# Expert biases as a float16 product of split weights, gelu rows handled by halves, and gate weights prepared one expert earlier

## What is computed

```
x = x + attention(layernorm(x))
h = layernorm(x)                                    # [tokens, 128]
gates = h @ router_w + router_b                     # 8 experts, the 2 best are kept
comb = softmax over those 2, zero for the others    # [tokens, 8]
shared = (sum over 2 experts of gelu(h @ sw1 + sb1) @ sw2 + sb2) / 2
moe = sum over 8 experts of comb[e] * (gelu(h @ w1[e] + b1[e]) @ w2[e] + b2[e])
x = x + shared + moe
```

## Time and profile before

| | us |
|---|---|
| median of 3 runs | 2149.64 |
| lowest and highest | 2147.13, 2152.54 |
| the profiled execution | 2150.59 |
| its span, first to last instruction | 2147.1 |
| PE busy in the span | 2082.1 (97%) |
| DVE, ACT, POOL busy | 1637.8, 1513.3, 1161.0 |

### The profile page before, as it was taken

One profiled execution on the slowest core, in us unless ns is written; L12 is line 12 of the kernel. 1 busy time (PEld: TensorE's weight loads), 2 busy tenths in 40 slices (PEclk: granted clock), 3 DMA queues, 4 the chain that ended last, 5 costly groups with the idle time before them and its releaser, 6 DMA issues.

```text
span 2147.1 us, 88171 instructions
## 1 busy us (share of the span) xinstructions
PE 2082.1 (97%) x37442; PEld 1544.8 (72%) x37442; DVE 1637.8 (76%) x3856; ACT 1513.3 (70%) x3304; POOL 1161.0 (54%) x1104
## 2 busy tenths in 40 slices
PE   3999999999999999999999999999998999999998
PEld 1777777777777777777777777777775777777776
DVE  4787787788778878977887787788875676677675
ACT  3666676666676676767666776766656888888887
POOL 5454546356354644544563455454415677777676
PEclk8999999999999999999999999999999999999999
DMA  5112211321221123123112211222112212212210
GB/s 139 33 55 66 74 55 45 86 65 54 62 79 55 45 66 81 49 59 89 48 53 66 75 55 55 76 62 58 44 55 23 30 20 24 29 20 24 29 20 11
DMA packets 255681, 114.48 MB, mean 53 GB/s; under 512 B 142218, under 2 KB 251156, under 8 KB 255348
## 3 DMA queue, kind: packets, MB, share of 16 engines
q1 hardware_dynamic: 255348, 109.60, 21.0%
HBM read 83.34 MB, written 8.39 MB: 43 GB/s over the span
## 4 chain that ended last, share of the span: by engine, by line
PE 84%; ACT 5%; POOL 4%; issue 3%; SPq 1%; DVE 1%; DMA 1%; ACTq 0%; POOLq 0%; DVEq 0%
PE ps L1276 21%; PE ps L1211 11%; PE ps L1296 10%; PE ps L1306 8%; PE ps L1218 8%; PE ps L1229 7%; POOL probs_t L545 3%; ACT probs L692 2%; PE ps L1458 2%; PE ps L1441 2%; PE ps L1443 2%; PE ps L1442 2%; PE ps L1460 2%; PE ps L1459 2%; PE ps L1314 1%
## 5 line engine op out<-in xcount | busy, mean ns | idle before, releaser
L624 ACT ACTIVATE probs<-ps,neg_max 128x512 f32<-128x512 f32 x1024 | 690.5, 686 | 352.2 <-DVE neg_max L819 352.1
L819 DVE TENSOR_REDUCE neg_max<-ps 128x1 f32<-128x512 f32 x1024 | 635.5, 682 | 151.7 <-PE ps L1218 147.3
L463 POOL TENSOR_TENSOR stat_hi<-q_twice,mask8h 128x1024 f16<-128x1024 f16 x128 | 242.8, 1897 | 659.1 <-PE ps L1218 594.2
L1276 PE MATMUL ps<-const,probs 128*128 128x128 f32 x4096 | 496.4, 274 | 0.7 <-ACT probs L624 0.6
L1276 PEld LDWEIGHTS ps<-const,probs 128*128 128x128 f32 x4096 | 453.4, 141 | 28.9 <-issue 15.5
L824 DVE COPY probs_t<-ps 128x512 f32<-128x512 f32 x512 | 339.5, 683 | 92.1 <-PE ps L1276 89.4
L545 POOL TENSOR_TENSOR probs_t<-probs,probs_t 128x1024 f16<-128x1024 f32 x160 | 340.1, 2134 | 108.8 <-ACT probs_t L698 108.8
L614 ACT ACTIVATE probs_t<-ps 128x512 f32<-128x512 f32 x512 | 278.6, 595 | 135.9 <-PE ps L1276 133.5
L1211 PE MATMUL ps<-keys,stat_hi 128*32 128x512 f16 x4096 | 318.0, 383 | 0.0
L1218 PE MATMUL ps<-rk_split,stat_rel 96*32 96x512 f16 (+2 forms) x4096 | 281.4, 340 | 0.0
L1025 DVE SCALAR_TENSOR_TENSOR keys<-ps,comb,keys 128x128 f32<-128x128 f32 x640 | 179.7, 343 | 128.7 <-PE ps L1460 128.6
(11 more groups left out here) (135 smaller groups left out, 2900.4 us busy)
## 6 DMA issues: line engine op xcount, KB each, us to landing
rv_step<-in_rv_win SPq DMA_DIRECT2D x128, 512.0 KB, 3.9
keys<-keys SPq DMA_DIRECT2D x64, 96.0 KB, 2.7
x_pair<-in_x SPq DMA_DIRECT2D x8, 512.0 KB, 4.6
q_twice<-q_hi SPq DMA_DIRECT2D x32, 128.0 KB, 2.9
q_lo_pair<-q_lo SPq DMA_DIRECT2D x32, 128.0 KB, 2.6
rel_scratch<-rel_t SPq DMA_DIRECT2D x256, 16.0 KB, 3.2
x_pair<-in_x SPq DMA_DIRECT2D x16, 256.0 KB, 3.1
x_pair<-rel_scratch SPq DMA_DIRECT2D x64, 64.0 KB, 3.9
```

Of the source, the lines that this page charges most:

```text
L624: nc.scalar.activation(probs[:, q, :], ps[:, i, :], ACT.Exp, bias=neg_max[:, q:q + 1], accum_out=row_sum[parity][:, s * QUADS + q:s * QUAD ...
L819: nc.vector.tensor_reduce(neg_max[:, q:q + 1], ps[:, i, :], op=ALU.max, axis=AX_X, negate=True).then_inc(max_done, 1)
L1276: last = nc.tensor.transpose(ps[:, bank, rt * P:(rt + 1) * P], probs[:, q, rt * P:(rt + 1) * P], ident)
```

## The change

1. The bias product is made in float16. `comb` and `b2_s`, both times 64, are split into high and low halves. `comb_split` holds high, low, high in three strips of 32 columns, `b2_split` high, high, low in three strips of 32 rows, so that one product of 96 rows gives the three terms. The transposes take float16 too. DVE divides by 64 where it adds the result.
2. `hidden` copies each half of 512 columns to float16 right behind its own gelu, and POOL subtracts half by half.
3. `down(0)` waits for expert 8 of the batch before, the last user of its bank, in place of expert 9, and `down(1)` for expert 9.
4. DVE's `prepare_comb` stands behind expert 6 in place of 7, and has two operations more.

```diff
 def low_rows(b, slot, e):
-    pool.wait_ge(hid_high, START + b * EXPERTS + e + 1)
     n = slot * EXPERTS + e
-    nc.gpsimd.tensor_tensor(hid_l[:, n % SLOTS, :, :], hid[:, n % 2, :, :], hid_h[:, n % SLOTS, :, :],
-                            ALU.subtract).then_inc(hid_low, 1)
+    for k in range(2):
+        pool.wait_ge(hid_high, START + b * 20 + e * 2 + k + 1)
+        nc.gpsimd.tensor_tensor(hid_l[:, n % SLOTS, k, :], hid[:, n % 2, k, :], hid_h[:, n % SLOTS, k, :],
+                                ALU.subtract).then_inc(hid_low, 1)
 def hidden(b, slot, e):
...
     for k in range(2):
         act.wait_ge(up_done, START + b * 20 + e * 2 + k + 1)
         nc.scalar.activation(hid[:, n % 2, k, :], ps[:, 4 + k, :], ACT.Gelu, bias=b1_s[:, e, k:k + 1],
                              scale=1.0 / W_SCALE).then_inc(gelu_done, 1)
-    act.wait_ge(down_done, SLOTS + b * EXPERTS + e - SLOTS + 1)
-    act.wait_ge(gelu_done, START + b * 20 + e * 2 + 2)
-    nc.scalar.activation(hid_h[:, n % SLOTS, :, :], hid[:, n % 2, :, :], ACT.Copy).then_inc(hid_high, 1)
+        if k == 0:
+            act.wait_ge(down_done, SLOTS + b * EXPERTS + e - SLOTS + 1)
+        act.wait_ge(gelu_done, START + b * 20 + e * 2 + k + 1)
+        nc.scalar.activation(hid_h[:, n % SLOTS, k, :], hid[:, n % 2, k, :], ACT.Copy).then_inc(hid_high, 1)
 # prepare_comb, on DVE
-    nc.vector.tensor_tensor(comb[:, slot, :, NS:], pick[:, :, 0, :], pick[:, :, 1, :], ALU.add).then_inc(comb_ready, 1)
+    link(nc.vector.tensor_tensor(comb[:, slot, :, NS:], pick[:, :, 0, :], pick[:, :, 1, :], ALU.add))
+    link.wait()
+    dve.wait_ge(comb_tr, START + b)
+    weights = comb[:, slot, :, :]
+    link(nc.vector.tensor_scalar(comb_split[:, :, 0:3:2, 0:EXPERTS], weights.unsqueeze(2).broadcast_to([P, TPB, 2, EXPERTS]),
+                                 W_SCALE, None, ALU.mult))
+    link.wait()
+    nc.vector.scalar_tensor_tensor(comb_split[:, :, 1, 0:EXPERTS], weights, W_SCALE, comb_split[:, :, 0, 0:EXPERTS],
+                                   ALU.mult, ALU.subtract).then_inc(comb_ready, 1)
 # second_biases, on DVE
-    nc.vector.tensor_tensor(acc[:, slot, :, :], ps[:, 3, :].rearrange("p (t d) -> p t d", t=TPB),
-                            acc[:, slot, :, :], ALU.add).then_inc(bias_added, 1)
+    nc.vector.scalar_tensor_tensor(acc[:, slot, :, :], ps[:, 3, :].rearrange("p (t d) -> p t d", t=TPB), 1.0 / W_SCALE,
+                                   acc[:, slot, :, :], ALU.mult, ALU.add).then_inc(bias_added, 1)
 # batch, on DVE
-                        if e == 7:
+                        if e == 6:
                             prepare_comb(b + 1, 1 - slot, link)
 # prepare_comb and second_biases, on PE
-    last = nc.tensor.transpose(ps[0:EXPERTS, 2, t * P:(t + 1) * P], comb[:, slot, t, :], ident)
+    halves_of = comb_split[:, t, :, :].rearrange("p a e -> p (a e)")
+    last = nc.tensor.transpose(bank_h(2, L)[0:3 * 32, t * P:(t + 1) * P], halves_of, identh[:])
-    last = nc.tensor.matmul(ps[:, 3, t * D:(t + 1) * D], comb_t[:, t * P:(t + 1) * P], b2_s[:], start=True, stop=True)
+    last = nc.tensor.matmul(ps[:, 3, t * D:(t + 1) * D], comb_t[:, t * P:(t + 1) * P], b2_split[:], start=True, stop=True)
 # down, on PE
-    pe.wait_ge(hid_low, SLOTS + b * EXPERTS + e + 1)
-    if e >= 2:
-        pe.wait_ge(y_used, START + b * (EXPERTS - 1) + e - 1)
+    pe.wait_ge(hid_low, SLOTS + b * 20 + e * 2 + 2)
+    if e == 1:
+        pe.wait_ge(final_ready, START + b)
     else:
-        pe.wait_ge(final_ready, START + b)
+        pe.wait_ge(y_used, START + b * (EXPERTS - 1) + max(e - 1, 0))
```

More of the change, by code:

```diff
@@ L194, in attention_ffn @@
         comb = sb("comb", [P, 2, TPB, EXPERTS])
-        comb_t = sb("comb_t", [EXPERTS, L])
+        comb_split = sb("comb_split", [P, TPB, 3, 32], F16)
+        comb_t = sb("comb_t", [3 * 32, L], F16)
+        b2_split = sb("b2_split", [3 * 32, D], F16)
         split = keys[0][:, 8 * L:12 * L].rearrange("p (a s c) -> p a s c", a=2, s=2)
@@ L241, in attention_ffn @@
         SETUP_DVE = 9
-        SETUP_POOL = 4
+        SETUP_POOL = 6
         STAT_OPS = 4
@@ L428, in _ @@
             nc.gpsimd.memset(comb[:], 1.0 / NS / W_SCALE).then_inc(setup_pool, 1)
+            nc.gpsimd.memset(comb_split[:], 0.0).then_inc(setup_pool, 1)
+            nc.gpsimd.memset(b2_split[:], 0.0).then_inc(setup_pool, 1)
             pool.wait_ge(setup_pool, SETUP_POOL)
@@ L686, in hidden @@
                 n = slot * EXPERTS + e
-                act.wait_ge(hid_low, SLOTS + b * EXPERTS + e - 1)
+                act.wait_ge(hid_low, SLOTS + b * 20 + e * 2 - 2)
                 for k in range(2):
@@ L712, in prepare_weights @@
                 act.wait_ge(comb_tr, START + b + 1)
-                nc.scalar.activation(comb_t[:], ps[0:EXPERTS, 2, :], ACT.Copy).then_inc(comb_t_ready, 1)
+                nc.scalar.activation(comb_t[:], bank_h(2, L)[0:3 * 32, :], ACT.Copy).then_inc(comb_t_ready, 1)
             for half in range(2):
@@ L942, in pair_steps @@
                         score_round(pair, parity, s, j, first, ahead)
-            FFN_LINKS = 14
+            FFN_LINKS = 16
             def prepare_attention(b, link):
@@ L1093, in _ @@
             dve.wait_ge(ffn_loaded, 16 * FFN_LOADS)
-            nc.vector.tensor_scalar(b2_s[:], b2_s[:], W_SCALE, None, ALU.mult).then_inc(w_low, 1)
+            for row in (0, 1):
+                nc.vector.tensor_scalar(b2_split[32 * row:32 * row + EXPERTS, :], b2_s[:], W_SCALE, None, ALU.mult).then_inc(w_low, 1)
+            dve.wait_ge(w_low, 4)
+            nc.vector.scalar_tensor_tensor(b2_split[64:64 + EXPERTS, :], b2_s[:], W_SCALE, b2_split[0:EXPERTS, :], ALU.mult, ALU.subtract).then_inc(w_low, 1)
             pair_steps(PAIRS - 1, 1, False, False)
@@ L1511, in _ @@
             pe.wait_ge(rel_t_ready, START + PAIRS * STEPS)
-            pe.wait_ge(w_low, 3)
+            pe.wait_ge(w_low, 5)
             for e in range(LOOK):
```

## The result

The changed kernel takes 2156.43 us in the median of 7 runs (2156.07 to 2159.16), the kernel before, run beside it, 2148.72 (2145.82 to 2152.54): ratio 1.0038 [1.0026, 1.0050], slower by 0.38%. The forecast was 2168, slower by 0.85% (against the 2149.64 of before). The profiled execution took 2156.08 us with a span of 2154.3, that is 5.5 and 7.2 us more than before. PE's busy time fell from 2082.1 to 2066.3 us while the span rose: PE has less work, and waits more.

The account below looks back on a forecast made before the run. PE was taken to bound the kernel, the other engines close behind. From 2150.6 us, -21 without the wait before `down(9)` and +38.5 with it, together +17, gave 2168; range 2128 to 2182.

Parts of the forecast that it names:

- Less PE work: Bias product 0.23 us instead of 1.17, gate-weight transposes 0.23 instead of 0.44: 1.15 us less PE work in a period.
- 0.6 before `down(4)`: A new PE wait of about 0.6 us before `down(4)`, for GpSimd's piece, gives back 0.6 of the 1.15.
- The queue behind GpSimd's halves: After expert 6, six VectorE operations of `prepare_comb` each wait for one GpSimd half, ending Z + 2.4 to Z + 8.6; chance 0.42.
- the wait before `down(9)`: PE waits for VectorE's expert 7: 3.4 us in 9 periods, 1.3 in 6 that cross a loop edge, +38.5 us.
- Z: End of GpSimd's second half for expert 7; from it, expert 7 ends at Z + 9.9, PE arrives at Z + 6.6.
- never catches up between experts 5 and 9: ScalarE with halves takes 2.64 us an expert, 30.1 a period, under PE's 30.4 + waits: no bound by itself.
- 6 x 1.3: In 6 periods crossing a loop edge, the two new operations slip through a GpSimd gap; `down(9)` waits 1.3 us each.
- hides its own 0.67: At loop edges, the 0.67 us PE wait from ScalarE's table load was taken as hidden, leaving a wait of 1.3.
- 1: Rival: VectorE's operations don't queue behind GpSimd's halves, so the whole gain stands, 2129 us; chance 0.27.
- 2: Rival: only the four old `prepare_comb` operations are held, 2149 us (chance 0.10); with one new one held, 2158 (0.10).
- 3: Rival: PE's idleness before `down(9)` costs its clock, 3 to 5 us each such stretch, up to 2200 us; chance 0.08.
- 4: Rival: ScalarE bounds if a half costs 0.05 more, at most +1 us a period; 2170, or 2140 without queue; no separate chance.

Follow-up runs that it names:

- e8: The e7 kernel with GpSimd's `deviations_after` behind `low_rows(4)` in place of `low_rows(3)`: 2143.33 us, 0.9966 of the kernel before.
- e1: The changed kernel with `prepare_comb`'s intermediates in PSUM bank 3 and one copy more: 2139.10 us, 0.9967 of the kernel before.
- e5: The kernel before with part 2 alone (ScalarE's copies and GpSimd's subtractions by halves): 2166.88 us, 1.0078 of the kernel before.
- e7: The changed kernel with `prepare_comb`'s values in PSUM and whole pieces instead of halves: 2136.13 us, 0.9930 of the kernel before.
- e6: The changed kernel with part 2 undone (whole pieces), parts 1, 3 and 4 kept: 2177.39 us, 1.0129 of the kernel before.

## Why the direction of the prediction was right, and its size wrong

- **Less PE work: right.** 0.22 and 0.22 us for product and transposes.
- **0.6 before `down(4)`: right,** 0.63. e8 adds that it is only moved by another order on GpSimd.
- **The queue behind GpSimd's halves: right,** all six held, both new ones too. e1 shows it: with the SBUF inputs in PSUM the same chain, one copy longer, takes 1.7 us.
- **The step that failed is one term of the sum, the wait before `down(9)`,** "9 x 3.4"; it is 2.0. Two things in it were wrong, the pace of the queue and the time at which PE arrives. Z is 1849.16 here (1846.77 + 2.39). The operations end at Z + 8.1 and not Z + 8.6, expert 7 at 1858.29, Z + 9.1 and not Z + 9.9: I took "1.14 us plus some 0.1 for VectorE's hold, 1.24" as the pace, but VectorE's turns cost GpSimd next to nothing (6.88 us for six, 1.147 each, against 6.74 for the six from 1838.95 on with no such turns). And PE would be there at 1855.04 + 1.31, Z + 7.2, not Z + 6.6.
- **Missed: a wait of 0.44 before `up(0)`,** which is most of that last difference. I said of ScalarE that it "never catches up between experts 5 and 9" and then priced it at nothing. e5 puts the halves alone at +17.9 us.
- **Right by luck: "6 x 1.3" for the loop-edge periods.** They took 32.48 instead of 32.33, but the wait of 1.3 before `down(9)` did not come at all. In its place stand the 1.37 us for ScalarE, of which the prediction said that the table load "hides its own 0.67". e1 and e7 confirm that: with nothing held they are still 32.48 with halves, and 31.49 with whole pieces.
- Together an ordinary period is 33.54 instead of 31.03 + 3.4 = 34.43. Eight of them give 7.1 us, the ninth, which took 32.35, another 2.1. The loop-edge periods give 0.9 back. That is 8.3 of the 10.3 us between the forecast span (2147.1 + 17.5) and the measured one; the start and the end of the kernel hold the rest. (The sum itself comes to 38.4 and not 38.5, and Z + 9.9 less Z + 6.6 to 3.3 and not 3.4; neither matters.)
- **Rivals.** 1 and 2 (no queue, only four held) did not happen. 3 did not either, at waits of 2.0 to 2.1, but did in e6 at 3.0; its "3 to 5 us" for each such stretch had no row behind it, and e6 shows 1.65. 4 happened, and without its condition: a half costs ScalarE 1.27, 0.05 less than I took and not 0.05 more, and it was not hidden everywhere, as said.

The parts do not add up. Alone, place, product and halves give +8.9, +1.6 and +17.9 us, 28.4 in sum, and the whole change +7.7. Place and product without halves give +28.5 (e6). So halves, a loss by themselves, win 21 us here. Of the 17.4 us between the two profiled spans (2171.7 and 2154.3) 10 are the clock's, and most of the rest is the shorter wait before `down(9)` (2.0 against 3.0). Why the halves cost less in company is argued from the timelines, and no run shows it by itself: PE already waits for others where ScalarE is late. Alone they put 0.64 inside `up(7)`; in the changed kernel nothing is left there, and a wait of 0.63 for GpSimd stands before `down(4)`, just ahead of it. Part 3, the other wait of `down(0)`, is in e6 as well, and wasn't tried alone.

## What to carry to other kernels

Before placing small VectorE operations, look at what GpSimd does in that moment: between SBUF tensors each can wait for a whole GpSimd instruction, so the six of 0.2 us here, queued one behind the other, took 6.6. If an idle PSUM bank is at hand, put their intermediates there. And when an engine's work per step nears the pace of the bound engine, as ScalarE's 2.54 us of halves did against PE's 2.65, it is no longer free, even at 83% busy (27.88 of 33.54): look at where it has extra pieces in a row and who waits behind them.

## What the hardware showed that I had not expected

- A held VectorE operation gets its turn at the seam between two back-to-back GpSimd instructions, and GpSimd loses almost nothing by it (six halves in 6.88 us with six such turns, in 6.74 without).
- RECIPROCAL is not held: 0.18 us in all 16 batches, and so in the midst of a GpSimd piece that held a TENSOR_SCALAR of the same 128x4 elements just before (0.81) and a TENSOR_TENSOR just after (0.86).
- Longer GpSimd pieces hold fewer operations for longer, and here the total is about the same, with gaps of 0.5 us between the pieces in which short operations slip through: 6.56 us from the first to the last of `prepare_comb` with halves, 7.1 with whole pieces.
- The part ahead of the expert stage differs from profile to profile by up to 9 us (first transposes of gate weights at 1631.4 to 1640.5) in kernels that hardly differ there. That is more than the whole effect of this change, so one profile of each would not have told 0.3%.
